# Moving the second halves of the key and receptance projections, and the shifted difference, within the pipelined loop of layer 1

## The reference, cut to what matters

```python
def _L0_xattn_ref(...): ...             # attention; its last step is a layernorm over axis 1
def _forward(x, state, ...):            # the second layer
    xa = _ln(x, ln1_w, ln1_b)
    sx = jnp.concatenate([state[:, i0 + 1][:, None], xa[:, :-1]], axis=1) - xa
    xxx = xa + sx * maa_x
    t = jnp.tanh(xxx @ maa_w1).reshape(B, L, 5, -1)
    mw, mk, mv, mr, mg = ...            # t times maa_w2, one each
    xk = xa + sx * (maa_k + mk)         # and xw, xv, xr, xg alike
    w = jnp.exp(-jnp.exp(time_decay + jnp.tanh(xw @ decay_w1) @ decay_w2))
    r, k, v = xr @ Wr.T, xk @ Wk.T, xv @ Wv.T
    g = jax.nn.silu(xg @ Wg.T)
    def step(s, inp):                   # s is 16 x 16 for each head
        a = k_l[..., :, None] * v_l[..., None, :]
        out = jnp.einsum('bhs,bhst->bht', r_l, faaaa * a + s)
        return a + w_l[..., None] * s, out
    y = scan(step over the 256 time steps)
    y = group norm of y over the 16 elements of a head
    x = x + y * g @ Wo.T
    xc = _ln(x, ln2_w, ln2_b)           # then the channel mix
    sxc = shifted xc - xc
    rr = jax.nn.sigmoid((xc + sxc * fmaa_r) @ fWr.T)
    kk = jnp.square(jax.nn.relu((xc + sxc * fmaa_k) @ fWk.T))
    return x + rr * (kk @ fWv.T)
```

## Time and profile before

| what | value |
|---|---|
| runs of the kernel before | 3673.56, 3679.35, 3684.85 us |
| the profiled execution's own time | 3673.02 us |
| its span, first to last instruction | 3671.2 us |
| mean granted TensorE clock | 0.959 of full |
| busy over the whole span | PE 93%, DVE 65%, ACT 45%, POOL 6% |
| layer 1's recurrence | first scan at 1503.9 us, last at 2346.0 us |
| scan of unit 0 of periods 0 to 7 starts at | 1503.9, 1601.3, 1714.2, 1827.1, 1939.3, 2052.6, 2166.2, 2271.2 us |

### The profile page before, as it was taken

The page is one execution under the profiler, slowest core; times in us unless marked ns, Lnnn a source line. Parts: engine busy times, 40 slices in busy tenths (PEclk is TensorE's granted clock), DMA queues, the critical chain, the costliest instruction groups (busy, mean ns, idle before and its releaser), DMA issues. The chain is left out here.

```text
span 3671.2 us, 53072 instructions
## 1 busy us (share of the span) xinstructions
PE 3398.8 (93%) x20600; PEld 2501.5 (68%) x20600; DVE 2386.1 (65%) x3835; ACT 1664.2 (45%) x3961; POOL 214.0 (6%) x311
## 2 busy tenths in 40 slices
PE   7999999999999995788988999679999999799998
PEld 6777887788787783555655566356666666478885
DVE  5666656666666662699898999726777777542212
ACT  4444444444444442345454454226666666532222
POOL 0000000000000000000000000001111110000000
PEclk9999999999999997889999999889999999999999
DMA  4333221221122203444343434230000000120004
GB/s 172 117 122 119 104 92 70 93 92 70 70 105 98 86 24 139 106 97 108 88 105 91 105 92 101 55 152 7 1 21 21 30 16 15 55 81 24 23 12 156
DMA packets 88952, 287.56 MB, mean 78 GB/s; under 512 B 19745, under 2 KB 27937, under 8 KB 64129
## 3 DMA queue, kind: packets, MB, share of 16 engines
q1 hardware_dynamic: 62576, 182.28, 16.8%
q0 software_dynamic: 10368, 75.50, 5.4%
q10 hardware_dynamic: 15760, 26.40, 2.1%
HBM read 229.63 MB, written 54.53 MB: 77 GB/s over the span
## 5 line engine op out<-in xcount | busy, mean ns | idle before, releaser
L453 ACT ACTIVATE l_prob<-l_bank,l_nmax 128x512 f32<-128x512 f32 x512 | 344.9, 686 | 281.5 <-DVE l_nmax L539 281.5
L539 DVE TENSOR_REDUCE l_nmax<-l_bank 128x1 f32<-128x512 f32 x512 | 317.6, 682 | 71.5 <-PE l_bank L373 71.4
L339 PE MATMUL l_bank<-l_x_hi,l_w_hi 128*128 128x256 f32 x1024 | 297.0, 290 | 16.0 <-DVE l_x_lo L598 16.0
L339 PE MATMUL l_bank<-l_x_hi,l_w_lo 128*128 128x256 f32 x1024 | 290.0, 283 | 0.0
L339 PE MATMUL l_bank<-l_x_lo,l_w_hi 128*128 128x256 f32 x1024 | 289.9, 283 | 0.0
L562 DVE COPY l_probT<-l_bank 128x512 f32<-128x512 f32 x256 | 173.8, 689 | 177.9 <-PE l_bank L387 176.5
L1562 DVE TENSOR_TENSOR_SCAN l_kv<-l_wx,l_kv 128x2056 f32<-128x2056 f32 x64 | 283.8, 4434 | 1.6 <-DVE l_nrs L1575 1.2
L2089 ACT ACTIVATE l2a_sc<-l2a_sc,l2a_nmax 128x256 f32<-128x256 f32 x512 | 254.0, 515 | 27.8 <-DVE l2a_nmax L2159 27.8
L387 PE MATMUL l_bank<-l_ident,l_prob 128*128 128x128 f32 x2048 | 252.0, 278 | 15.2 <-DVE l_k_lo L555 10.6
L387 PEld LDWEIGHTS l_bank<-l_ident,l_prob 128*128 128x128 f32 x2048 | 229.7, 143 | 28.7 <-DVE l_k_lo L555 20.8
L409 PE MATMUL l_bank<-l_probT,l_v 128*64 128x512 f32 x1024 | 233.8, 598 | 0.0
(11 more groups left out here) (287 smaller groups left out, 7633.7 us busy)
## 6 DMA issues: line engine op xcount, KB each, us to landing
l_vb<-vd SPq DMA_DIRECT2D x64, 1024.0 KB
l_w_hi<-kept_w_hi POOLq DMA_DIRECT2D x24, 1024.0 KB, 8.3
l_w_lo<-kept_w_lo POOLq DMA_DIRECT2D x24, 1024.0 KB, 10.2
l_wv_hi<-kept_wv_hi POOLq DMA_DIRECT2D x12, 1024.0 KB, 5.1
l_wv_lo<-kept_wv_lo POOLq DMA_DIRECT2D x12, 1024.0 KB, 7.1
l_wraw<-in_l_wqk SPq DMA_DIRECT2D x8, 1024.0 KB, 8.5
kept_w_hi<-l_w_hi SPq DMA_DIRECT2D x8, 1024.0 KB, 10.7
kept_w_lo<-l_w_lo SPq DMA_DIRECT2D x8, 1024.0 KB, 12.5
```

Source lines behind the costliest of these rows:

```text
L339: mm = pe.matmul(s.ap[:, c * ROWS:(c + 1) * ROWS], a[:, kt, c, g, :], b[:, kt, c * ROWS:(c + 1) * ROWS], start=m == 0, stop=m == 3 * KT - 1)
L453: act.activation(prob[h][:, it, :], s.ap[:, :], ACT.Exp, bias=nmax[:, n % 2, it, h:h + 1], accum_out=rsum[:, n % 2, it, h:h + 1]).then_inc ...
L539: dve.tensor_reduce(nmax[:, n % 2, it, h:h + 1], s.ap[:, :], AX.X, ALU.max, negate=True).then_inc(max_ready, 1)
```

## The change

`ring`, PE, ACT and DVE lists are reordered; no instruction is added or removed.

- PE: project of p keeps only half 0 of k and of r at its old place. Half 1 of k of batch element b comes in the next period after `centre`, half 1 of r after picks of unit 8b; `spread_rs` moves behind `first`.
- ACT: half 0 of r is evicted after the next period's `normed`; half 1 of k between `squares` and `roots`; `first_part` moves ahead of the eviction of half 1 of r, `spread_w`, `store` and `start_state`. `normed_c` moves ahead of `mixture` w.
- DVE: `shift` moves from behind the second scan to the end of slot 0, ahead of that scan, in the place of `bonus_rk`, which moves to the end of slot 1. `first_input` moves from behind the spread of slot 1 to directly behind its scan. `bonus_v` and `gate_y` change places.

```diff
         ring += [f"xT{p}_0", f"xT{p}_1"] if p is not None else []
-        ring += [f"cen{c}_0", f"cen{c}_1", f"var{c}", f"rsb{c}_0", f"rsb{c}_1"] if c is not None else []
-        ring += [f"t{p}", f"mv{p}_0", f"mv{p}_1"] if p is not None else []
+        ring += [f"cen{c}_0", f"cen{c}_1"] if c is not None else []
+        ring += [f"k{r}_1"] if r is not None else []
+        ring += [f"var{c}"] if c is not None else []
+        ring += [f"r{r}_1"] if r is not None else []
+        ring += [f"t{p}"] if p is not None else []
+        ring += [f"rsb{c}_0", f"rsb{c}_1"] if c is not None else []
+        ring += [f"mv{p}_0", f"mv{p}_1"] if p is not None else []
...
-        ring += [f"k{p}_0", f"k{p}_1"] if p is not None else []
+        ring += [f"k{p}_0"] if p is not None else []
         ring += [f"fv{c}_0", f"fv{c}_1"] if c is not None else []
-        ring += [f"r{p}_0", f"r{p}_1"] if p is not None else []
+        ring += [f"r{p}_0"] if p is not None else []
...
                     if c >= 0:
                         centre(c)
+                    if now:
+                        project(b, "k", (1,))
+                    if c >= 0:
                         variances(c)
                     if now:
                         picks(PER * b)
-                    if c >= 0:
-                        spread_rs(c)
+                        project(b, "r", (1,))
                     if 0 <= p < B:
...
                         first(p)
+                    if c >= 0:
+                        spread_rs(c)
+                    if 0 <= p < B:
                         mixture(p, "v")
...
-                        project(p, "k")
+                        project(p, "k", (0,))
...
-                        project(p, "r")
+                        project(p, "r", (0,))
...
                         normed(p)
                     if now:
                         if b:
-                            act.wait_ge(z_ready, PER * b)
-                            act.wait_ge(ruk_ready, b)
-                        project(b, "r", 1, ir)
+                            act.wait_ge(z_ready, PER * (b - 1) + 4)
+                        project(b, "r", 0, ir)
...
                     if c >= 0:
                         squares(c)
+                    if now:
+                        if b:
+                            act.wait_ge(kv_ready, PER * b)
+                        project(b, "k", 1, ik)
+                    if c >= 0:
                         roots(c)
+                    if 0 <= p < B:
+                        first_part(p)
                     if now:
+                        if b:
+                            act.wait_ge(z_ready, PER * b)
+                        project(b, "r", 1, ir)
                         spread_w(b, 1)
                     if c >= 1:
                         store(c - 1)
                     if now:
                         start_state(PER * b + 2)
                     if 0 <= p < B:
-                        first_part(p)
                         tanh(p)
...
                         store_v(p)
-                        mixture(p, "w")
                     if c >= 0:
                         normed_c(c)
+                    if 0 <= p < B:
+                        mixture(p, "w")
...
                         if p:
                             act.wait_ge(ruk_ready, p)
-                        for half in H2:
-                            if p:
-                                act.wait_ge(kv_ready, PER * (p - 1) + 4 * (half + 1))
-                            project(p, "k", half, ik)
+                            act.wait_ge(kv_ready, PER * (p - 1) + 4)
+                        project(p, "k", 0, ik)
                         start_state(PER * p)
                         spread_w(p, 0)
-                        if p:
-                            act.wait_ge(z_ready, PER * (p - 1) + 4)
-                        project(p, "r", 0, ir)
...
                         if n == 1 and 0 <= p < B:
-                            shift(p)
+                            first_input(p)
                         if n == 1 and c >= 0:
                             inverse(c)
+                        if n == 2 and now:
+                            bonus_v(b)
                         if n == 2 and c >= 0:
                             gate_y(c)
-                        if n == 2 and now:
-                            bonus_v(b)
...
                             spread(unit + 1)
-                        if n == 1 and 0 <= p < B:
-                            first_input(p)
...
                             receive(unit)
-                        if n == 0 and now:
+                        if n == 0 and 0 <= p < B:
+                            shift(p)
+                        if n == 1 and now:
                             bonus_rk(b)
```

More of the change, by code:

```diff
@@ L999, in bonus, with columns @@
                         mm.then_inc(s.full, 1)
-                def columns(label, weight, src):
-                    for half in H2:
+                def columns(label, weight, src, own=H2):
+                    for half in own:
                         s = S[f"{label}_{half}"]
@@ L1053, in mixture, with project @@
                         mm.then_inc(s.full, 1)
-                def project(p, n):
+                def project(p, n, own=H2):
                     if p == 0:
@@ L1058, in project @@
                     pe.wait_ge(xf_ready, input_count(p, n))
-                    columns(f"{n}{p}", W["W" + n], xf[INPUTS.index(n) % 2])
+                    columns(f"{n}{p}", W["W" + n], xf[INPUTS.index(n) % 2], own)
                 def decay_in(p):
@@ L1751, in _ @@
                 chain.close()
+NH, HD = 16, 32
+QUAD = P // HD
 NH, HD = 16, 32
```

## The result

The changed kernel takes 3623.7 us (median of 4 executions, 3621.25 to 3627.21) against 3678.62 us for the kernel before beside it (median of 4): ratio 0.9851, 95% interval 0.9833 to 0.9868. Run again later beside seven executions of the kernel before (3679.34), it gave 3618.73 us, ratio 0.984 (0.9825 to 0.9855). So the gain was 55 us in the first comparison and 61 in the second. The forecast was 3626 us, with a range of 3612 to 3652.

What follows compares the result with a forecast made beforehand. Order, not load, was taken to bound the kernel: PE and DVE wait for each other. Removing 51 us of waits gave 3622 from the profiled execution, 3628 from the median; 3626 was taken, range 3612 to 3652.

Steps and rivals of the forecast that it cites:

- lost by order and not by load: Loop periods: PE and DVE each 91% busy in period 2, waiting for each other in turn; without DVE's waits, about 104.3 us.
- the sum: DVE's waits for PE, 51.8 us, and 0.4 for `first_input`, about 1 us kept: gain 51 us; a period about 104.3.
- 55 us off the lowest execution: Reason given for the lower end, 3612 us, of the forecast's own range 3612 to 3636.
- The offsets: Predicted times of steps in a period, counted from T, the start of its scan 0, using old durations.
- `shift` ahead of scan 1: DVE, slot 0: would wait 1.9 us if `turned` stayed at T+10.6; `turned` was expected by about T+2.7, so no wait.
- PE gains 2.85: PE's `turn` to xc: with `normed_c` ahead of `mixture` w on ACT, its 2.85 us wait goes, at no cost.
- The rule on the most-contended engine: Trainium skill: weight-load busy share, here 60%, measures TensorE's headroom; read so, the change brings nothing, 3673 us.
- A: Rival, 22 in 100: PE stays late by a little, two more clock dips giving waits of 2 to 3.5 us a period; 3644.
- B: Rival, 4 in 100: waits only move, to `bonus_v` (1.9 us) and a late `fv`; gain under 11 us, 3672.
- C: Rival, 3 in 100: slower, as `shift` blocks scan 1 when `turned` is late; at T+20 in six periods +16, 3692.
- D: Rival, 2 in 100: the change doesn't do what it says, halves held by a bank or by `ik`, `ir`; 3673.
- The 1 us kept for `bonus_v` of period 0: DVE's wait at `bonus_v` in period 0, 4.0 us before, was expected to keep about 1 us, as PE starts it cold.

## Why the prediction was right, and where it was not

**The bound.** That time was lost by order and not by load held. The waits for PE went from 51.8 to 0.2 us, and the loop fell by 53.2. The period is 104.0 us where the sum had 104.3. The sum counted waits alone, 51 us; DVE's busy time over the loop, which it held to be unchanged, fell a little too, from 779.8 to 777.1 us. That DVE bounds is shown from both sides: 25.6 us of added work cost all of it and more, 15.9 us taken away gave 9.9. The time was forecast as 3626, between a sum taken from the profiled execution (3622) and one from the median (3628). The two medians, 3623.7 and 3618.73, are closer to the first or under it, so the last few us of agreement are luck. In the range, "55 us off the lowest execution" is 3618.6 and not 3612; the bound stood lower than its own reason puts it.

**The offsets.** `first` at T+15.6 (forecast 15.5), `bonus` T+24.2 to T+26.2 (24.2 to 26.1), `normed_c` done T+50.4 (50.3), `spread_deviations` done T+67.9 (67.9), `fv` done T+97.9 (97.6). One was off: PE waited only 0.2 us for receive 0 in period 2, since half 0 of r ended at T+1.4 and not T-1.8. Three stretches at half rate in the period before, where PE was busy 103.50 of 104.03 us, are the likely reason. In period 3, after a period with one short stretch, PE did wait there, 1.57 us.

**The halves.** Right, and shown alone (22.4 us on the loop) and undone (28.2).

**`shift` ahead of scan 1.** I wrote that it would wait 1.9 us if `turned` stayed where it was. With the halves back it waited up to exactly 1.9 us, and moving it then brought little or nothing. So the one part brings its full worth only with the other. The prediction priced this as a rival's condition and not as a term, which was enough for the sum.

**`normed_c`.** The mechanism was right, and "PE gains 2.85" is the gap alone. On the kernel before, the step brought 26.2 us on the loop of one execution (24 by the medians, 13 to 29 by the interval). In that execution periods 1 to 5 fell by 3.2 to 7.3 us each and periods 0 and 6 did not fall, and PE's busy time fell with the stretches at half rate. The total was right all the same, because DVE bounds at 104 us and what PE gains beyond that is not seen.

**The clock.** I wrote that I take little from the rule of the Trainium skill (TensorE: Matmul & The Clock Gate, The HAM clock gate) that an idle engine brings the clock down. The runs bear it out in part. With the 2.85 us gap filled the mean clock of all five middle periods rose, in one of them to 1.00. But in the period before that one the clock fell after 3.60 us without any idle time on PE; there the trace does not agree. The theory behind the run without the one-column products, that they help to bring the fall on, was not borne out either: there the mean clock of periods 2 to 5 did not rise.

**The rule on the most-contended engine** (the Trainium skill, Perfetto Trace Analysis, Identifying the Most-Contended Engine) would have had PE 40% free and the change worth nothing. Here 3.55 us of added PE work a period cost 2.4 us at the end of the period and 1.2 in its first third (16.9 and 8.6 over seven, by the loop), so PE's queue was nearly full, as its matmul busy share says and its weight loads do not. As a measure of distance from peak the rule isn't tested here.

**Rivals.** A was right in kind: margins are a few us; the two runs with PE work added show about 1.1 us a period hidden at the end and 2.3 in the first third. It did not happen, and not for want of half clock: over periods 1 to 5 the mean clock was 0.93, 0.98, 0.95, 0.95 and 0.95 (before: 0.89 to 0.95), and even at 0.93 and 103.50 us of busy time PE came early enough. B, C and D did not happen; no wait was found at L1617 and none at `bonus_v`. The 1 us kept for `bonus_v` of period 0 wasn't needed either: that period fell by 4.6 us, forecast 3.5.

What stays open: why the clock falls in one period and not in the next of the same kernel, and what brings it down. And since `normed_c` alone was seen in one profiled execution, the size of its part beyond the gap is not settled.

## What to carry to other kernels

When two engines are each about 90% busy and wait for each other, look in each for where it idles, and move work that isn't urgent out of the stretch in front of the other's waits into that idle stretch: here 7 us of work a period moved 8 to 18 us later, at no cost in work. Price such moves together, since one may bring most of its worth only with another: the same reordering of `normed_c` was worth 26 us on the loop alone and 12 as the last step. When two engines are both nearly full, add work to one and then to the other to see which sets the time; the busy shares, 98% and 99% here, did not tell. Small reorderings that close a recurring idle gap are worth trying by themselves; the cheapest edit here, two steps exchanged on ScalarE, brought nearly half of the gain when it stood alone.

## What was not expected of the hardware

- The same 494 matmul records took 97.78 us in a period at granted clock 1.00 and 102.67 us in the one ahead of it at 0.95, in one execution of one kernel.
- In the period at 0.95 the clock fell from full to half while PE was busy without a gap (3.60 of 3.60 us before the fall, 6.80 of 6.80 after it).
- Taking work off TensorE did not raise the clock: without 15 of the 16 one-column records the mean of period 2 was 0.92 against 0.94, with a new stretch of 6.8 us at half rate elsewhere.
- An addition of two 128x1024 operands takes 1.22 us on VectorE. On GpSimd it took, as the profile has it, 6.11 us when it began under a VectorE scan, and 2.17 us the one time (of eight) that VectorE had nothing to do. The scan took its usual 4.43 us; the VectorE product that began before the addition had ended took 2.71 us and not 2.29.
